# Queries and keys as two float32r pieces instead of three bf16 ones, in an attention, FFN and mixer kernel

## The reference

```python
c_kv = x @ W_kv_down
k = (c_kv @ W_k_up).reshape(Bb, Tt, NH, HD)          # NH, HD = 16, 16
v = (c_kv @ W_v_up).reshape(Bb, Tt, NH, HD)
q = (x @ W_q).reshape(Bb, Tt, NH, HD)
scores = jnp.einsum('bqhd,bkhd->bhqk', q, k)
scores = scores + jnp.einsum('bqr,bkr->bqk', q_rope, k_rope)[:, None]
scores = jnp.where(causal, -jnp.inf, scores / scale)
attn = jnp.einsum('bhqk,bkhd->bqhd', softmax(scores), v).reshape(Bb, Tt, D_MODEL)
```

## Time and profile before

| | us |
|---|---|
| median of 3 runs | 1405.07 |
| lowest and highest | 1403.31 and 1408.92 |
| profiled execution, span | 1405.9 |
| TensorE busy | 1216.6 |
| VectorE busy | 1089.1 |
| ScalarE busy | 1052.2 |
| GpSimd busy | 333.9 |
| first and last score matmul start | 45.2 and 1141.8 |

### The profile page before, as it was taken

How to read it: one execution, slowest core, us unless ns; L and a number is a source line. 1 busy time by engine, 2 the same in 40 slices (tenths; PEclk the granted TensorE clock), 3 DMA queues, 4 the chain that set the end, 5 groups by cost and what they waited for, 6 DMA issues and landing times.

```text
span 1405.9 us, 23146 instructions
## 1 busy us (share of the span) xinstructions
PE 1216.6 (87%) x8060; PEld 778.2 (55%) x8060; DVE 1089.1 (77%) x2259; ACT 1052.2 (75%) x2103; POOL 333.9 (24%) x317
## 2 busy tenths in 40 slices
PE   5889885999899988998799989999899988977347
PEld 2575653465556754675556755666566655534224
DVE  3683388788788979889788989898688988887830
ACT  4675788797959878797859888788949887458522
POOL 3944110520133102320124112310133110510101
PEclk9799996999999999999999999999999999998669
DMA  8504141514142123521333041523151140031100
GB/s 254 113 9 102 27 130 42 115 31 116 46 102 72 23 75 88 126 46 41 98 91 82 24 128 28 132 44 103 38 120 38 26 131 28 23 96 50 37 0 15
DMA packets 72084, 101.65 MB, mean 72 GB/s; under 512 B 10640, under 2 KB 44064, under 8 KB 71968
## 3 DMA queue, kind: packets, MB, share of 16 engines
q1 hardware_dynamic: 71968, 100.16, 27.3%
HBM read 74.44 MB, written 25.69 MB: 71 GB/s over the span
## 4 chain that ended last, share of the span: by engine, by line
PE 54%; DVE 16%; ACT 16%; issue 6%; POOL 5%; SPq 1%; DMA 1%; POOLq 0%; DVEq 0%; ACTq 0%
PE ps L873 19%; PE ps L883 15%; PE ps L956 5%; DVE work L1516 4%; ACT work L1203 4%; PE ps L1042 4%; DVE work L1439 3%; PE ps L974 3%; PE ps L948 3%; ACT work L1210 3%; DVE work L1507 2%; ACT xnd L1146 2%; DVE work L1525 2%; PE ps L865 1%; DVE work L1394 1%
## 5 line engine op out<-in xcount | busy, mean ns | idle before, releaser
L1516 DVE TENSOR_TENSOR_SCAN work<-work 128x512 f32<-128x512 f32 x256 | 313.1, 1255 | 39.5 <-ACT work L1270 37.8
L1203 ACT ACTIVATE work<-work 128x384 f32<-128x384 f32 (+3 forms) x512 | 264.4, 559 | 54.6 <-DVE work L1439 52.7
L1439 DVE CUSTOM_DVE_ANT_0 work<-ps,work 128x384 f32<-128x384 f32 (+3 forms) x512 | 228.0, 486 | 90.8 <-PE ps L948 87.0
L752 POOL TENSOR_TENSOR later_norms<-later_norms,singles 128x2 f32<-128x2 f32 x112 | 97.0, 867 | 768.9 <-ACT xnd L1146 465.4
L956 PE MATMUL ps<-ident,work 128*128 128x128 f32 x1280 | 203.4, 285 | 21.4 <-DVE work L1439 10.2
L956 PEld LDWEIGHTS ps<-ident,work 128*128 128x128 f32 x1280 | 151.8, 145 | 84.5 <-issue 35.3
L1210 ACT COPY work<-ps 128x512 f32<-128x512 f32 x300 | 169.9, 573 | 7.8 <-PE ps L956 7.3
L1525 DVE TENSOR_TENSOR work<-work 128x1024 f32<-128x1024 f32 x128 | 160.0, 1250 | 4.3
L948 PE MATMUL ps<-work 96*128 96x384 bf16 (+3 forms) x512 | 124.1, 310 | 38.7 <-ACT work L1210 32.1
L873 PE MATMUL ps<-led_xTd,wf 128*128 128x512 f32 x256 | 120.3, 621 | 3.9 <-issue 3.9
L873 PE MATMUL ps<-led_xTd,wfc 128*128 128x512 f32 x256 | 118.0, 596 | 0.0
(11 more groups left out here) (176 smaller groups left out, 1950.7 us busy)
## 6 DMA issues: line engine op xcount, KB each, us to landing
work<-values SPq DMA_DIRECT2D x64, 256.0 KB, 3.1
work<-ratios SPq DMA_DIRECT2D x64, 256.0 KB, 3.2
scratch<-work SPq DMA_DIRECT2D x32, 384.0 KB, 4.7
work<-scratch SPq DMA_DIRECT2D x64, 192.0 KB, 3.9
work<-scratch SPq DMA_DIRECT2D x64, 128.0 KB, 4.2
x_in<-x SPq DMA_DIRECT2D x8, 512.0 KB, 6.7
work<-scratch SPq DMA_DIRECT2D x64, 64.0 KB, 4.3
values<-work SPq DMA_DIRECT2D x16, 256.0 KB, 3.2
```

The costliest lines, as they stand in the source:

```text
L1203: i = s_.activation(part_of, part_of, ACT.Exp, scale=-1.0, bias=nmax[:, row:row + 1])
L1439: i = v_.tensor_tensor_reduce(sc[:, n % 4, at:at + nk], out_of(b, name)[:, at:at + nk], base_of(qt), -SCORE_SCALE, BIG, ALU.add, ALU.min, ...
L1516: v_.tensor_tensor_scan(ring[:, at, m, :], pwr[:, slot, :], ring[:, at, m, :], 0.0, ALU.mult, ALU.add).then_inc(*scanned.one)
```

## The change

Queries and keys are split into two pieces of type float32r (4 bytes): ScalarE's copy, and VectorE's subtraction, which now writes the second piece itself. GpSimd's two steps for each half are gone. A head then needs three products of pieces, 3 x 16 = 48 rows. Two heads lie above each other, at partitions 0 to 47 and 64 to 111; two more lie beside them in the free dimension. The matmul of a head reads only its own rows.

```diff
-RUNS = (((0, 3), (0, 3)), ((0, 2), (1, 2)), ((0, 1), (2, 1)))
-SROWS = 6 * HD
+SROWS = 3 * HD
+SGROUP = P // 2
-         [((1, j, 0), (1, j + 1, 2 * P)) for j in (0, 2)])
+         [((1, j, 0), (1, j + 2, 2 * P)) for j in (0, 1)])
...
-        words = 28864
+        stack = ctx.enter_context(nc.sbuf_tensor("stack", [P, 2, 2, 2, T], F32R))
+        words = 24768
...
-        k_pieces = part(3 * DC * T // 2).bitcast(BF16).rearrange("p (c s t) -> p c s t", s=3, c=DC)
+        k_pieces = part(2 * DC * T).bitcast(F32R).rearrange("p (c s t) -> p c s t", s=2, c=DC)
-        rest = xna[:].rearrange("p t d -> p (t d)").rearrange("p (c t) -> p c t", c=DC)
+        q_pieces = [a.bitcast(F32R).rearrange("p (s t) -> p s t", s=2)
+                    for a in (xna[:].rearrange("p t d -> p (t d)"), base[:, 0:2 * T])]
...
             def load_group(b, hg):
-                i, at = hg % 2, 0
-                for run in RUNS:
-                    for kind in range(2):
-                        s0, k = run[kind]
-                        sp.dma_start(stack[at:at + k * HD, i, kind].rearrange("p j t -> p (j t)"),
-                                     scratch[b, kind, hg % 2, hg // 2, s0:s0 + k]
-                                     .rearrange("s (d j) t -> (s d) (j t)", j=4)).then_inc(*stacked[i].one)
-                    at += k * HD
+                i = hg % 2
+                for kind in range(2):
+                    for h in range(2):
+                        sp.dma_start(stack[h * SGROUP:h * SGROUP + SROWS, i, kind].bitcast(F32).rearrange("p j t -> p (j t)"),
+                                     scratch[b, kind, hg, h, 0:SROWS].rearrange("r j t -> r (j t)")
+                                     ).then_inc(*stacked[i].one)
...
                 if item == "pieces":
-                    need(sp, third_piece, b, (n + 1) * DC)
-                    pieces = (q_pieces, k_pieces)[n]
-                    for half in range(2):
-                        r = half * 64
-                        sp.dma_start(scratch[b, n, half].rearrange("c s r t -> r (c s) t"),
-                                     pieces[r:r + 64].rearrange("p c s t -> p (c s) t")).then_inc(*pieces_sent.one)
+                    for c in range(DC):
+                        is_drained(sp, b, f"{'qk'[n]}{c}")
+                        pieces = k_pieces[:, c] if n else q_pieces[c]
+                        for to, of, k in [(0, 0, 1), (1, 0, 2)] if n == 0 else [(0, 0, 2), (2, 0, 1)]:
+                            rows = scratch[b, n, 2 * c:2 * c + 2, :, to * HD:(to + k) * HD].rearrange(
+                                "g h (s d) j t -> (g h) (d j) s t", s=k)
+                            for s0 in range(k):
+                                sp.dma_start(rows[:, :, s0], pieces[:, of + s0].bitcast(F32)).then_inc(*pieces_sent[n].one)
...
-                if item in ("q", "k"):
-                    pieces, pick = (q_pieces, (1, 2)) if item == "q" else (k_pieces, (1, 0))
-                    is_drained(pool, b, f"{item}{n}")
-                    pool.sem_inc(waits_taken, 1)
-                    g_.tensor_copy(pieces[:, n, pick[0], :], rest[:, n, :]).then_inc(*second_piece.one)
-                    need_given(pool, second_piece)
-                    g_.tensor_tensor(pieces[:, n, pick[1], :], rest[:, n, :], pieces[:, n, pick[0], :],
-                                     ALU.subtract).then_inc(*third_piece.one)
...
                     for qt, j, at in TILES[n % UNITS]:
                         nk = (qt + 1) * P
-                        i = mm(out_of(b, name)[:, at:at + nk], stack[0:SROWS, hg % 2, 0, j, qt * P:(qt + 1) * P],
-                               stack[0:SROWS, hg % 2, 1, j, 0:nk], start=True, stop=True)
+                        of = stack[j % 2 * SGROUP:j % 2 * SGROUP + SROWS, hg % 2, :, j // 2]
+                        i = mm(out_of(b, name)[:, at:at + nk], of[:, 0, qt * P:(qt + 1) * P], of[:, 1, 0:nk], start=True, stop=True)
...
-                if first:
-                    need(dve, third_piece, b, n + 1)
-                v_.tensor_tensor(rest[:, n, :], out_of(b, f"{kind}{n}"), piece[:, n, :], ALU.subtract
+                v_.tensor_tensor(pieces[:, 1, :], out_of(b, f"{kind}{n}"), pieces[:, 0, :].bitcast(F32), ALU.subtract
...
                 if item == "base":
                     name, at = f"base{n}", n * P
+                    if n == 0:
+                        need(dve, pieces_sent[0], b, 3 * DC)
```

```diff
-        "a5 p a3 p a6 p4 a34 p a24 p a31 p3 a6 p a p a p a p a p a5 d a2 d a2 d a4 d6 a3 d a6 d a3 d a6 d a12 "
+        "a8 p a2 p a4 p4 a32 p a4 p a30 p2 a9 p a7 p a7 p a p a3 p a2 p a9 d a3 d a d2 a3 d a d2 a3 d a3 d a3 d "
```

More of the change, by code:

```diff
@@ L10 @@
 I32 = mybir.dt.int32
-BF16 = mybir.dt.bfloat16
+F32R = mybir.dt.float32r
 P = 128
@@ L161 @@
            "osum gystats ternary prep tables means late",
-    "pool": "stats q k ystats fstats fc fystats zstats oystats gstats gystats gsum ternary tables late",
+    "pool": "stats ystats fstats fc fystats zstats oystats gstats gystats gsum ternary tables late",
     "sp": "fetch pieces group z kv ratio rates pw inv gsum",
@@ L168 @@
     "pe":
[11 rows of a table removed]
-    "act":
[16 rows of a table removed]
-    "dve":
[13 rows of a table removed]
[12 rows of a table added]
+    "act":
[16 rows of a table added]
+    "dve":
[14 rows of a table added]
     "pool":
[2 rows of a table removed]
+        "a p9 a3 d17 a3 d14 a3 d22 a d2 a d a d19 a d3 a2 d19 a3 d22 a d3 a2 d23 a2 d34",
     "sp":
[3 rows of a table removed]
+        "a3 d a10 d a d2 m8 d2 m5 a3 m a2 m3 a2 d2 m d m2 d m10 a5 m a m3 d3 a d3 m8 d m5 a5 m a m3 d3 a d2 m4 "
+        "d m4 d m5 a5 m a m3 d3 a d2 m4 d m4 d m5 a5 m a m3 d3 a d3 m4 d m9 a5 m4 d a d2 a d2 m d m6 d m9 d m "
+        "d5 m4 d m13 d4",
 }
@@ L400, in part @@
             return ap.rearrange(f"p ({' '.join(names)}) -> p {' '.join(names)}", **dict(zip(names, shape)))
-        stack_at = cut[0]
-        stack = part(2 * 2 * 4 * T // 2).bitcast(BF16).rearrange("p (i k j t) -> p i k j t", i=2, k=2, j=4)
-        cut[0] = stack_at + 2 * 4 * T // 2
-        q_pieces = part(3 * DC * T // 2).bitcast(BF16).rearrange("p (c s t) -> p c s t", s=3, c=DC)
-        cut[0] = stack_at + 2 * 2 * 4 * T // 2
         base = part(TT * (TT + 1) // 2 * P)
@@ L457, in sandwich_kernel @@
         first_piece = signal("first_piece", 2 * DC)
-        second_piece = signal("second_piece", 2 * DC)
-        third_piece = signal("third_piece", 2 * DC)
-        pieces_sent = signal("pieces_sent", 4, 16)
-        stacked = [signal(f"stack{i}_loaded", 2 * 2 * len(RUNS), 16) for i in range(2)]
+        pieces_sent = [signal(f"{kind}_pieces_sent", 3 * DC, 16) for kind in "qk"]
+        stacked = [signal(f"stack{i}_loaded", 2 * 2 * 2, 16) for i in range(2)]
         exped = signal("exped", ALL)
@@ L686, in do @@
                 if item == "pieces":
-                    need(sp, third_piece, b, (n + 1) * DC)
-                    pieces = (q_pieces, k_pieces)[n]
-                    for half in range(2):
-                        r = half * 64
-                        sp.dma_start(scratch[b, n, half].rearrange("c s r t -> r (c s) t"),
-                                     pieces[r:r + 64].rearrange("p c s t -> p (c s) t")).then_inc(*pieces_sent.one)
+                    for c in range(DC):
[6 more added lines that the diff above has]
+                                sp.dma_start(rows[:, :, s0], pieces[:, of + s0].bitcast(F32)).then_inc(*pieces_sent[n].one)
                 if item == "group":
                     if n < 2:
-                        need(sp, pieces_sent, b, 4)
+                        need(sp, pieces_sent[0], b, 3 * DC)
+                        need(sp, pieces_sent[1], b, 3 * DC)
                     else:
@@ L943, in do @@
                     if n % UNITS == 0:
-                        need(pe, stacked[hg % 2], b, (hg // 2 + 1) * 2 * len(RUNS))
+                        need(pe, stacked[hg % 2], b, (hg // 2 + 1) * 4)
                     may_fill(pe, b, name)
@@ L1188, in do @@
                     is_filled(act, b, f"q{n}")
-                    s_.copy(q_pieces[:, n, 0, :], out_of(b, f"q{n}")).then_inc(*first_piece.one)
+                    s_.copy(q_pieces[n][:, 0, :], out_of(b, f"q{n}")).then_inc(*first_piece.one)
                 if item == "k":
                     is_filled(act, b, f"k{n}")
-                    s_.copy(k_pieces[:, n, 2, :], out_of(b, f"k{n}")).then_inc(*first_piece.one)
+                    s_.copy(k_pieces[:, n, 0, :], out_of(b, f"k{n}")).then_inc(*first_piece.one)
                 if item == "v":
@@ L1378, in copied, with split @@
                 v_.tensor_copy(dst, src).then_inc(*drains(b, name))
-            def split(b, kind, n, piece, first):
+            def split(b, kind, n, pieces, first):
                 need(dve, first_piece, b, first + n + 1)
-                if first:
-                    need(dve, third_piece, b, n + 1)
```

(10 more changed lines are left out.)

## The result

The changed kernel takes 1690.07 us (median of 4 runs, 1687.06 to 1699.29) against 1405.51 for the kernel before on the same chip: 1.203 times as long, interval 1.199 to 1.207. The direction was forecast, the size not: the time lies 252 us above the forecast of 1438 and 202 us above the end of the range. Some executions fall in a slower state with a lower granted clock, and all times here are those of fast ones: only e8 had slow ones, two of four (1503.78, which is the profiled one, and 1505.34 us, beside 1479.97 and 1498.55).

A forecast was written before the change was run, and what follows sets the result against it. TensorE, dense in the attention loop, was taken as the bound: 1405.9 + 25.7 (shape changes) + 7 (DMA waits) = 1438.6 us of span, so 1438 us forecast, range 1390 to 1488.

The forecast's parts named there:

- the DMA term: Doubled bytes of the pieces' sends make scores wait 0 to 3 us in each of 7 batches: 7 us, bounds 0 and 21.
- 3.15 MB take 13 us: A batch's twelve sends of pieces move at the full DMA rate, about 243 GB/s.
- second rival: Sends in many pieces run below 243 GB/s, scores wait 5 us a batch: 28 us more, 1466 us; chance 0.10.
- The added wait: VectorE's base 0 copy waits for the queries' six sends: some 1 us, covered by idle time; uncovered, 8 us in all.
- The shape term: 48-row score matmuls bring 535 more shape changes on TensorE at 0.09 us: 48.2 us, 38.6 after deductions.
- The share that reaches the end: Idle time in the main stretch takes a third of TensorE's added 38.6 us; two thirds, 25.7 us, reach the end.
- The stream at 0: float32r score matmuls move columns at the bf16 price: 0 us added, bounds 0 and 68.
- the first rival: float32r scores stream at the fp32 record's rate, TensorE gets 68 us more: 1484 us; chance 0.13, full fp32 0.02.
- GpSimd and the latency at nothing: GpSimd's dropped casts and subtractions (25.0 + 38.9 us), and 2.0 us less latency from last key to sends, alone gain nothing.
- The orders at nothing: The new instruction orders got no term, though TensorE's work from key products to first score falls from 22.8 to 15.5 us.
- work moved behind the scores is not saved: TensorE work that the new order puts after a batch's first scores instead of ahead of them gains nothing.
- Batch 0: In the first batch, earlier sends and doubled bytes cancel for the scores' wait: -4.5 to +4.5 us, taken as 0.

The follow-up runs named there:

- e8: e1 with ScalarE's two sine operations turned into exponentials, so that the function table changes no more in the loop: 1489.26 us, ratio 1.059.
- e2: The kernel before, bf16 pieces and its own orders, score matmuls on 48 rows instead of 96, half the products of pieces left out: 1447.64 us, ratio 1.030.
- e3: e1 with the float32r score matmuls over rows 0 to 111, the array's full height, adding two heads' scores: 1442.08 us, ratio 1.026.
- e1: The changed kernel with scratch rows laid out so that a send's outermost DRAM dimension is 64 instead of 4: 1497.48 us, ratio 1.065.
- e9: e1 with the order tables of the kernel before, and ScalarE's two sine operations turned into exponentials: 1467.87 us, ratio 1.044.

## Why the prediction was wrong

**What failed is the DMA term.** The step "3.15 MB take 13 us" took the rate of a full set of engines, 243 GB/s, for sends whose shape is not that of the sends in those rows: before, the outermost dimension was 64 (64x6x512), after, 4 (4x32x512), and both stand in the fence on SyncE's order ahead of the prediction. Measured: 102.5 GB/s, 30.7 us a batch. What follows hangs on it: the scores' wait was 12 us a batch, not 1. The prediction's second rival names the mechanism (sends slower than 243 GB/s) and gave it 5 us a batch, 28 us; the price was 193.

**The added wait** was traced rightly (base 0, what is queued behind it, who waits) and sized at 1 us covered or 8 uncovered. It was 91.7 us of VectorE and 75.4 of TensorE. It hangs on the same rate: with sends over all engines it is 4.4 us, once.

**The shape term was right in kind, too small in size.** The count was right: the traces have 302 neighbours of unlike shape before and 837 after, 535 more. 0.09 us a change is what the earlier trace rows show, and e2 has it at 0.10. Missing were 0.05 us in the second transpose of each turn, and the 0.11 us an item that 4-byte operands cost in this shape, by their weights as far as the starts tell. TensorE's added time in e2 is 56 us, where 48.2 was the high end and 38.6 the value. The share that reaches the end, two thirds by choice, was 43 of 56 us in e2; from e3 to e1 it was 55 of 72 us by the medians of the times, but 42 of 72 by the two profiled runs from which the 72 are taken. So it lies between 0.6 and 0.8, and two thirds was well chosen, though nothing had measured it.

**The stream at 0 was right** (0.149 against 0.147 us for 128 columns), and the first rival falls: that some measured times lie near its 1484 is not the stream's doing. What the Trainium skill ("FP8 and Floating Point Precision", TensorE Precision Notes) states, four passes for true FP32, and a reading of 4 bytes with truncation for reduced precision, agrees with these columns.

**GpSimd and the latency at nothing**: nothing speaks against it. No run tests the 63 us less work of GpSimd by itself; whatever it brought is within the 11 us left over.

**The orders at nothing** was wrong by 21 to 28 us. The step "work moved behind the scores is not saved" looked at one head of a batch only. The 40 more table loads could have been foreseen from the order of ScalarE, but they cost nothing.

**Batch 0** had been set even, -4.5 to +4.5. Its first scores start at 69.4 us in the changed kernel and at 45.2 before, 24 us later; in e1 at 43.8. The earlier sends did win 1.4 us there, once they ran on all engines.

**The sum, redone** with measured parts: 1405 + 11 (left over) + 53 (shape, with the unhidden load) + 28 (orders) + 193 (sends) = 1690. It comes out exactly because each part is the step from one kernel to the next. With the sends over all engines the prediction's 1438 would have stood against 1497, outside the range as well: 28 us by the orders, 27 by the shape with its weight load (53 against 25.7), 4 by the rest (11 against 7).

## What to carry to other kernels

Where an edit reshapes a DMA, read the outermost dimension of both of its sides ahead of the bytes: a full rate read from other transfers of the trace is no bound for it, and a slow send holds its queue and whatever waits for it. A matmul that leaves the shape of its neighbours costs both ways and in the matmul after, here 0.25 us a turn, so using half of the rows paid nothing with scores between transposes. A table of orders is a part of the change like any other, and needs a price, or at least a range.

## What the runs showed of the hardware

- With 4, 8, 16 and 64 as the outermost dimension of 256 KB sends the DMA engines moved 102, 191, 291 and 336 GB/s at shares of 0.26, 0.52, 0.91 and 0.89, and a send with others ahead of it occupied the queue for 2.44, 1.25, 0.71 and 0.61 us; the first three of a batch took 0.56 us even at 4.
- A change to half of the rows cost 0.10 us in, 0.10 us out, and 0.05 us between the next two matmuls (e2).
- float32r streamed at the rate of bf16 (0.149 and 0.207 us against 0.147 and 0.200 behind scores of 128 and 256 columns), while its weight load was recorded with 202 ns against 99. An item cost 0.11 us more in 48 rows, 0.02 in the full shape.
- Of the 17 pairs of adjacent score items in the two row groups 9 started 2 to 4 ns apart, so they ran side by side; the other 8, the second and third of three in a row, started 0.59 us apart (0.33 in e1). The parallelism exists, and this order used 9 places for it.
- Table loads taken out of ScalarE, 91 us of them in e8 and 39 in e9, moved the time by 8 and 2 us, within the intervals, though ScalarE had been 75% and 72% busy.
